# Decoder layer: ScalarE normalises all four tiles of a half in the later norms; shared experts start in the last norm; weights, route rows and down projections in a new order

## What is computed

```python
x = x + attn(layernorm(x))          # 16 heads, delta rule over 256 steps, conv, gate, Wo
x = x + xattn(layernorm(x), ctx)    # softmax(ctx Wq . ctx Wk) applied to the features
x = x + ffn(layernorm(x))           # the part that the change is about, below

scores = sigmoid(h @ gate_weight.T)                # 16 routed experts
topk_idx = best 4 of (scores + bias) within the best 2 of 4 groups
weight = scores[topk] / sum * 2.5
routed = sum over n of weight[t, n] * ((silu(h @ gate_w[n].T) * (h @ up_w[n].T)) @ down_w[n].T)
out = routed + (silu(h @ sh_gate.T) * (h @ sh_up.T)) @ sh_down.T
```

## Time and profile before

| | us |
|---|---|
| median of three runs | 598.18 |
| the profiled execution | 597.41 |
| its span, first to last instruction | 595.5 |
| TensorE busy | 557.4 (94%) |
| VectorE, ScalarE, GpSimd busy | 437.1, 398.3, 298.9 |
| mean granted TensorE clock | 0.991 |

### The profile page before, as it was taken

How to read it: one execution, slowest core, us unless ns; L and a number is a source line. 1 busy time by engine, 2 the same in 40 slices (tenths; PEclk the granted TensorE clock), 3 DMA queues, 4 the chain that set the end, 5 groups by cost and what they waited for, 6 DMA issues and landing times.

```text
span 595.5 us, 10331 instructions
## 1 busy us (share of the span) xinstructions
PE 557.4 (94%) x3392; PEld 488.2 (82%) x3392; DVE 437.1 (73%) x1046; ACT 398.3 (67%) x783; POOL 298.9 (50%) x201
## 2 busy tenths in 40 slices
PE   3899999999999999999999999897777799999996
PEld 1687889989989989989989988786566688888885
DVE  8778989989989988998998998968593433333334
ACT  4978988878978979879779778665531433343331
POOL 2434756746746646656666563301041655556542
PEclk9998999999999999999999999999998899999999
DMA  6122032032032032032031020110002433333311
GB/s 206 29 107 81 0 117 81 1 116 81 2 117 81 2 116 81 2 116 75 8 116 56 27 97 23 59 29 1 0 1 70 149 105 107 104 123 113 108 62 70
DMA packets 16267, 42.23 MB, mean 71 GB/s; under 512 B 4544, under 2 KB 4800, under 8 KB 16224
## 3 DMA queue, kind: packets, MB, share of 16 engines
q1 hardware_dynamic: 16224, 41.69, 20.9%
HBM read 40.47 MB, written 1.21 MB: 70 GB/s over the span
## 4 chain that ended last, share of the span: by engine, by line
PE 83%; DVE 8%; ACT 4%; DMA 2%; issue 2%; SPq 1%; ACTq 0%; DVEq 0%
PE bank L1258 20%; PE bank L1260 19%; PE bank L1259 19%; PE bank L1254 15%; PE bank L1396 5%; PE bank L1384 4%; ACT tok L624 2%; DMA xbias<-in_xb 1%; DMA w_raw<-in_w 1%; DVE stats L976 1%; DVE xT_lo L911 1%; DVE gated_lo L1158 1%; ACT values L538 0%; DVE x L1248 0%; DVE raw L995 0%
## 5 line engine op out<-in xcount | busy, mean ns | idle before, releaser
L1258 PE MATMUL bank<-xT_lo,w_hi 128*128 128x512 f32 x336 | 140.0, 417 | 3.6 <-DVE conv L1149 1.3
L1260 PE MATMUL bank<-xT_hi,w_hi 128*128 128x512 f32 x336 | 132.3, 394 | 0.0
L1259 PE MATMUL bank<-xT_hi,w_lo 128*128 128x512 f32 x336 | 131.8, 392 | 0.0
L425 POOL TENSOR_TENSOR gated_lo<-gated,gated_hi 128x512 fp32r<-128x512 f32 x30 | 38.7, 1290 | 116.5 <-ACT gated_hi L644 112.8
L624 ACT ACTIVATE tok<-bank,nmr,rstd 128x128 f32<-128x128 f32 x256 | 91.0, 504 | 2.1 <-DVE nmr L891 2.1
L502 POOL TENSOR_TENSOR gate<-conv,tap 128x512 f32<-128x512 f32 x36 | 46.4, 1291 | 84.5 <-DVE conv L1149 71.4
L1258 PEld LDWEIGHTS bank<-xT_lo,w_hi 128*128 128x128 f32 x336 | 63.5, 189 | 18.8 <-DVE conv L995 3.2
L1260 PEld LDWEIGHTS bank<-xT_hi,w_hi 128*128 128x128 f32 x336 | 63.3, 188 | 14.2
L420 POOL TENSOR_TENSOR conv<-tap,conv 128x506 f32<-128x506 f32 x32 | 61.9, 1934 | 21.8 <-DVE conv L995 21.8
L420 POOL TENSOR_TENSOR raw<-tap,raw 128x506 f32<-128x506 f32 x32 | 61.9, 1934 | 20.3 <-DVE raw L995 16.3
L1259 PEld LDWEIGHTS bank<-xT_hi,w_lo 128*128 128x128 f32 x336 | 63.7, 190 | 9.6
(11 more groups left out here) (167 smaller groups left out, 1358.3 us busy)
## 6 DMA issues: line engine op xcount, KB each, us to landing
w_raw<-in_w SPq DMA_DIRECT2D x34, 384.0 KB, 4.4
obet<-obet_rows SPq DMA_DIRECT2D x16, 768.0 KB, 4.2
tap<-route_rows SPq DMA_DIRECT2D x16, 512.0 KB, 3.6
wv_raw<-in_wv SPq DMA_DIRECT2D x8, 256.0 KB, 4.8
wo_raw<-in_wo SPq DMA_DIRECT2D x8, 256.0 KB, 4.9
x<-in_x SPq DMA_DIRECT2D x2, 512.0 KB, 4.6
out_x<-x SPq DMA_DIRECT2D x4, 256.0 KB, 2.4
raw<-in_ctx SPq DMA_DIRECT2D x1, 512.0 KB, 5.4
```

The lines of the kernel that those rows point to most:

```text
L425: nc.gpsimd.tensor_tensor(gated_lo[:, cc], gated[:, c * N:(c + 1) * N], gated_hi[:, cc].bitcast(F32), ALU.subtract).then_inc(gated_lo_read ...
L1258: nc.tensor.matmul(o, l_hi, r_lo, start=start, stop=False, skip_group_check=loose)
L1259: nc.tensor.matmul(o, l_lo, r_hi, start=False, stop=False, skip_group_check=loose)
L1260: return nc.tensor.matmul(o, l_hi, r_hi, start=False, stop=stop, skip_group_check=loose)
```

## The change

- In norms 2 and 3 (i = 1, 2) `half_norm` writes all four tiles of a half on ScalarE, none on VectorE.
- The second half's two energies get banks of their own (6 and 7), and their maxima and exponentials move behind the first half's norm. `context_recip` of the second half stays ahead of that half's norm factors on VectorE.
- Experts 3 and 4 get their split weights early, in buffers that are free by then (`early_high` on ScalarE ahead of the second half's softmax, `early_low` on GpSimd after the first mix has been added). Experts 5 and 6 take the two ordinary slots, which SyncE loads as soon as these are free. GpSimd then does nothing until the router chain is over (`r_ready`).
- The shared experts aren't multiplied by ones any more; their product goes straight to `act_high`.
- Activations are kept in two buffers, and `down(n)` stands two experts behind `gate_up(n)`; the first half of the shared experts' gate and up stands among the last norm's steps.
- In the loop, ScalarE and GpSimd split the gate and up weights of expert n + 1 and the down weights of expert n in step n. SyncE loads gate and up weights (256 KB) and down weights (128 KB) apart, in the order gate/up of n + 2, route row of n, down of n + 2.

The three `early`, `two` and `e_bank` helpers only pick addresses: the buffers for experts 3 and 4, the half of a double buffer by the parity of n, and the bank. `e_count(n, c)` numbers the chunks, since the shared experts' chunks run in another order.

```diff
@@ -358,35 +384,55 @@
+            for n in (5, 6):
+                sp.wait_ge(w_lo_ready, n - 2 + H)
+                load_expert(n, 1 - n % 2)
             sp.wait_ge(r_tr_ready, NCH)
             sp.dma_start(route_rows, routeT).then_inc(ld["route_rows"], 16)
             sp.wait_ge(ld["route_rows"], 16)
 
-            def load_route(e, s, before):
-
-                sp.wait_ge(e_weighted, before)
+            def load_route(e, s):
+
+                if not (isinstance(e, int) and e < 2):
+                    sp.wait_ge(e_weighted, e * NCH - NCH)
                 sp.dma_start(wbc[:, s * T:(s + 1) * T],
                              route_rows[bass.ds(e, 1), :].broadcast_to([P, T])).then_inc(ld_route[s], 16)
 
+            def load_gate_up(n, s):
+
+                sp.wait_ge(w_lo_ready, n + (H - 2))
+                m = n + (H - 1)
+                sp.dma_start(w_raw[:, s * 3 * D:s * 3 * D + 2 * D],
+                             w_in[bass.ds(m, 1), :, 0:2 * D].rearrange("a p c -> (a p) c")).then_inc(ld_w[s], 16)
+
+            def load_down(n, s):
+                sp.wait_ge(down_lo_ready, n - 6)
+                m = n + (H - 1)
+                sp.dma_start(w_raw[:, s * 3 * D + 2 * D:(s + 1) * 3 * D],
+                             w_in[bass.ds(m, 1), :, 2 * D:3 * D].rearrange("a p c -> (a p) c")
+                             ).then_inc(ld_down[s], 16)
+
+            load_route(0, 0)
+            load_route(1, 1)
+            load_gate_up(7, 0)
+            load_route(2, 0)
+            load_down(7, 0)
+            load_gate_up(8, 1)
+            load_route(3, 1)
+            load_down(8, 1)
+            with sp.Fori(0, E_ROUTED // 2 - 3) as r:
+                for s in range(2):
+                    load_gate_up(r * 2 + (9 + s), s)
+                    load_route(r * 2 + (4 + s), s)
+                    load_down(r * 2 + (9 + s), s)
             for s in range(2):
-                load_route(s, s, NCH * (s + 1))
-            with sp.Fori(0, E_ROUTED // 2 - 1) as r:
...
-            def weigh(n, s, first):
-
-                for c in range(NCH):
-                    pool.wait_ge(u_prod, (n - 1) * NCH + c + 1)
-                    if not first:
-
-                        pool.wait_ge(e_hi, (n - 2) * NCH + c + 1)
-                        pool.wait_ge(e_lo, (n - 2) * NCH + c + 1)
-                    cc = slice(c * N, (c + 1) * N)
-                    nc.gpsimd.tensor_tensor(act_w[:, cc], prod[:, cc], wbc[:, s * T + c * N:s * T + (c + 1) * N],
-                                            ALU.mult).then_inc(e_weighted, 1)
-
-
-
-            pool.wait_ge(p_added, TT // 2)
-            nc.gpsimd.memset(wbc, 1.0).then_inc(ones_ready, 1)
-            pool.wait_ge(ones_ready, 1)
-            weigh(1, 0, True)
-            gate_up_low(3, 0)
-            weigh(2, 1, False)
-            gate_up_low(4, 1)
-            down_low(3, 0)
-
-            def step(n, s, left=2):
-
-                pool.wait_ge(ld_route[s], (n - 1 - s) * 8)
-                weigh(n, s, False)
-                if left > 1:
-                    gate_up_low(n + 2, s)
-                if left > 0:
-                    down_low(n + 1, 1 - s)
-
-            with pool.Fori(0, E_ROUTED // 2 - 1) as r:
+            def early_low(n):
+                hi, lo = early(n)
+                s = 1 - n % 2
+                pool.wait_ge(w_hi_ready, n + H)
+                nc.gpsimd.tensor_tensor(lo, w_raw[:, s * 3 * D:(s + 1) * 3 * D], hi.bitcast(F32),
+                                        ALU.subtract).then_inc(w_lo_ready, 1)
+
+            def weigh(n, m, s, c):
+
+                pool.wait_ge(u_prod, n * NCH + (c + 1 - NCH))
+                if not (isinstance(n, int) and n < 5):
+
+                    pool.wait_ge(e_hi, n * NCH + (c + 1 - 3 * NCH))
+                    pool.wait_ge(e_lo, n * NCH + (c + 1 - 3 * NCH))
+                nc.gpsimd.tensor_tensor(weighted(m, c), prod[:, two(m, c)],
+                                        wbc[:, s * T + c * N:s * T + (c + 1) * N],
+                                        ALU.mult).then_inc(e_weighted, 1)
+
+
+            pool.wait_ge(x_mixed, 1)
+            early_low(3)
+            early_low(4)
+
+            pool.wait_ge(r_ready, 1)
+            gate_up_low(5, 0)
+            gate_up_low(6, 1)
+
+            def step(n, m, s, up=True, down=True):
+                pool.wait_ge(ld_route[s], n * 8 - (1 + s) * 8)
+                weigh(n, m, s, 0)
+                if up:
+                    gate_up_low(n + 1, 1 - s)
+                weigh(n, m, s, 1)
+                if down:
+                    down_low(n, s)
+
+            step(3, 3, 0, False, False)
+            step(4, 4, 1, False, False)
+            step(5, 5, 0, False)
+            step(6, 6, 1)
+            with pool.Fori(0, E_ROUTED // 2 - 3) as r:
                 for s in range(2):
-                    step(r * 2 + (3 + s), s)
-            step(E_ALL - 1, 0, 1)
-            step(E_ALL, 1, 0)
+                    step(r * 2 + (7 + s), 7 + s, s)
+            step(E_ALL - 1, E_ALL - 1, 0)
+            step(E_ALL, E_ALL, 1, False)
...
                 act.wait_ge(ln_rstd, NCH * i + c + 1)
-                for t in (G * c, G * c + 1):
+
+                for t in range(G * c, G * c + (2 if i == 0 else G)):
                     nc.scalar.activation(x_norm[:, t * D:(t + 1) * D], x[:, t * D:(t + 1) * D],
                                          ACT.Identity, scale=rstd[:, t:t + 1],
...
 
             act.wait_ge(ld["router"], 32)
             nc.scalar.activation(rw_hi, rw, ACT.Copy).then_inc(small_split, 1)
             context_soft(0)
-            context_exp((4, 5))
             context_att(0)
             half_norm(1, 0)
+            half_out(1, 0, xT)
+            context_exp((4, 5))
             context_exp((6, 7))
-            half_out(1, 0, xT)
+            early_high(3)
+            early_high(4)
             context_soft(1)
             context_att(1)
             half_norm(1, 1)
             half_out(1, 1, xT)
-            for c in range(NCH):
-                half_norm(2, c)
...
-            def step(n, s, left=2):
-                gate_silu(n, False)
-                if left > 1:
-                    gate_up_high(n + 2, s)
-                act_high(n, False)
-                if left > 0:
-                    down_high(n + 1, 1 - s)
-
-            with act.Fori(0, E_ROUTED // 2 - 1) as r:
+            def step(n, m, s, up=True):
+                gate_silu(n, m)
+                if up:
+                    gate_up_high(n + 1, 1 - s)
+                act_high(n, m)
+                down_high(n, s)
+
+            gate_silu(4, 4)
+            act_high(3, 3)
+            gate_silu(5, 5)
+            act_high(4, 4)
+            act_high(5, 5)
+            down_high(5, 0)
+            step(6, 6, 1)
+            with act.Fori(0, E_ROUTED // 2 - 3) as r:
                 for s in range(2):
-                    step(r * 2 + (3 + s), s)
-            step(E_ALL - 1, 0, 1)
-            step(E_ALL, 1, 0)
...
-            def norm_half(i, c):
+            def norm_half(c):
                 norm_factors(G, D, G * c).then_inc(ln_rstd, 1)
-                half_norm(i, c)
 
             gated_out(g, k, 0)
+            context_recip(0)
+            add_stats((0, 1), p_full, p_acc, p_added)
+            gated_out(g, k, 1)
+            norm_half(0)
             context_max(2)
-            context_recip(0)
-            add_half(0, p_full, p_acc, p_added)
-            gated_out(g, k, 1)
-            norm_half(1, 0)
             context_max(3)
-            add_half(1, p_full, p_acc, p_added)
+            add_stats((2, 3), p_full, p_acc, p_added)
             context_recip(1)
-            norm_half(1, 1)
+            norm_half(1)
             dve.wait_ge(small_split, 2)
             nc.vector.tensor_tensor(rw_lo, rw, rw_hi.bitcast(F32), ALU.subtract).then_inc(r_lo_ready, 1)
-            add_half(0, x_mix_full, mix_acc, x_mixed)
-            norm_half(2, 0)
-            add_half(1, x_mix_full, mix_acc, x_mixed)
+            add_stats((0, 1), x_mix_full, mix_acc, x_mixed)
+            norm_half(0)
+            add_stats((2,), x_mix_full, mix_acc, x_mixed)
             half_low(2, 0)
-            norm_half(2, 1)
+            add_stats((3,), x_mix_full, mix_acc, x_mixed)
+            norm_half(1)
+
...
             def half_transpose(i, c):
 
-                pe.wait_ge(ln_norm_act, 2 * (NCH * i + c + 1))
-                pe.wait_ge(ln_norm_dve, 2 * (NCH * i + c + 1))
+                if i == 0:
+                    pe.wait_ge(ln_norm_act, 2 * (c + 1))
+                    pe.wait_ge(ln_norm_dve, 2 * (c + 1))
+                else:
+                    pe.wait_ge(ln_norm_act, TT // 2 + G * (NCH * (i - 1) + c + 1))
                 for kt in range(KT):
...
             half_transpose(1, 0)
-            mix(0)
+            mix(0, (0, 1))
             context_weights(1)
             half_transpose(1, 1)
-            mix(1)
+            mix(1, (2,))
+            half_transpose(2, 0)
```

(68 more changed lines are left out.)

224 lines of the change are left out of this document (128 added, 96 removed).

## The result

| | before | after |
|---|---|---|
| median of the runs, us | 598.18 | 627.64 (3 runs, 624.64 to 627.73) |
| profiled execution: time / span, us | 597.4 / 595.5 | 624.64 / 622.9 |
| mean granted clock of TensorE | 0.991 | 0.977 |
| TensorE's busy time, share of the span | 557.4 us, 94% | 568.0 us, 91% |

The changed kernel is slower: ratio 1.0469, 95% interval 1.0386 to 1.0553. I had forecast 620 us and a range of 606 to 633.

A forecast was written before the change was run, and what follows sets the result against it. TensorE bound the old kernel; the exposed route row would bound the new loop. `down_low(5)` at 465.3, 11 turns of 11.5 to 591.8, then the last matmuls and tail: 618.8, plus 1.9 outside the span, 620.7; forecast 620 us, range 606 to 633.

The forecast's parts named there:

- its length: Router chain: falls from 19.2 to 12.2 us, 5.7 from GpSimd being idle and 1.3 from expert chunks moved out.
- `down_low(5)` ends: Before the loop: first route row, weighing, expert 5's row, rounding and both splits put this end at 465.3 us.
- R: In the loop, from the end of `down_low` to the route row's landing: 5.3 us, between 4.4 and 6.6.
- second `weigh`: GpSimd's last `weigh` in a loop step: 1.29 us, plus 0 to 0.7 for an `act_low` between, taken as 0.2.
- turn: Loop cycle between `down_low` ends: 11.5 us (10.4 to 13) where TensorE needs 8.28, repeated 11 times.
- from there to the end of the span: After the loop: 5.3 + 2.65 to `gate_up(18)`, 5.5 + 3 x 2.8 of matmuls, 1.6 slow start, 3.5 tail.
- The price of the page: Loop transfers by the skill page: 4.1 us rather than 5.1, cycle 10.5, result about 609, still inside the range.
- this stage gives nothing to the router (0.4 later): Norms and cross attention: the router chain begins at 432.3 us against 431.96, with one quarter more of gate/up done.
- rival D: TensorE's clock in the loop: pauses absorb a low clock; at 1.2 GHz throughout, the kernel takes 689 us; 3%.
- all 5.7 of the old excess: Router chain: seven long VectorE instructions each go beside a GpSimd one; with GpSimd idle there, 5.7 us go.
- A: Loop, faster: the route row lands in time, TensorE's work bounds again, experts 8.28 us apart, 581 us; 7%.
- C: Middle: VectorE's long instructions stay or ScalarE's four tiles cost more; `down_low(5)` ends 6 us later, 626; 10%.

The follow-up runs named there:

- route_early: Changed kernel with each route row issued one place earlier in SyncE's list, no longer behind the transfer that waits for the other expert's down half: 585.28 us, ratio 0.9786.
- before_late: Kernel before, with each route row issued on SyncE behind the transfer that waits for its own down-projection half: 633.44 us, ratio 1.0571.
- early_split: route_early with the tiles of the two later norms shared again, two on ScalarE and two on VectorE: 581.31 us, ratio 0.9733.
- pool_late: Changed kernel with GpSimd's two wide subtractions for experts 3 and 4 started with the router's scores, beside the router's chain: 634.99 us, ratio 1.0619.
- split_again: early_split measured once more, unchanged, with more rounds and beside the next kernel on one chip: 582.36 us, ratio 0.9733.
- tuned: early_split with ScalarE's two wide copies moved later and GpSimd's two wide subtractions placed anew among VectorE's norm ops: 578.67 us, ratio 0.9675.

## Why the prediction was right, step by step

**What decides it** held as put: the route row issued only behind `down_low`, first thing needed by the next step. route_early removes it and gives 585; before_late adds it and gives 633.

| step | forecast | measured |
|---|---|---|
| router's chain begins | 432.3 | 434.74 |
| its length | 12.2 | 12.2 |
| `down_low(5)` ends | 465.3 | 468.10 |
| end of `down_low` to the first `weigh` (R) | 5.3 | 5.37 at 484.27; mean 5.5 |
| second `weigh` | 1.29 + 0 to 0.7 | 1.74 |
| turn | 11.5 | 11.70 |
| `down_low(16)` ends | 591.8 | 596.77 |
| from there to the end of the span | 27.0 | 26.1 |
| span | 618.8 | 622.9 |

The 4.1 us between the spans are 2.8 before the loop, 2.2 in eleven turns of 0.2 each, less 0.9 at the end. The median, 627.64, lies 7.6 above the 620 that I forecast, because it is also 3.0 above the profiled execution from which these rows come.

The signs mostly held: a wait for the row in every turn, experts 11 to 12 apart, TensorE waiting in the loop for nothing but `gate_up_low`, and no op of the chain over 1 us. Two were a little off: TensorE was 79% busy from 475 to 600 (98.58 of 125 us), where I had said 72%, and the row was issued 1.35 after `down_low`'s end, where I had said 1.2 at most.

**The loop.** R was mis-sized by a little. I gave an issue 0.4; in the loop issues are 0.5 to 0.7 apart (478.93, 479.62, 480.25), and the landing behind the row's own is 3.7 to 4.2 in these two turns. Both errors cancel, which is luck: from the first issue to the landing I had 5.1, and it took 5.0 in this turn (478.93 to 483.96) and 5.3 in the next. The 0.3 from the landing to the start of `weigh` (483.96 to 484.27) I had left out. R's mean over the 12 waits behind a `down_low` is 5.5 for my 5.3; the first of the 13 waits for a row, 6.5, stands ahead of the loop. The second `weigh` takes 0.4 to 0.5 more than the first in every turn, beside an `act_low` that starts 0.5 before it and is itself longer (1.08 for 0.69): inside my 0 to 0.7.

**The price of the page.** By an estimate from the Trainium skill, DMA: Bandwidth & Descriptors, "Anatomy of one DMA", three transfers of 896 KB in all would have landed 4.1 behind the first issue. They took 5.0 to 5.3: the trace doesn't agree, and 1.3 of that are the two issues ahead of the row, which stand in no figure of one DMA.

**Before the loop.** The step "this stage gives nothing to the router (0.4 later)" failed by 2.4 us. The order of events was as I had it, and even some things came sooner (the reciprocal at 405.38, for my 406.8). What I left out is TensorE's low clock here; I had priced it behind the last wait and, as rival D, in the loop. It fell around a wait of 2.69 us for ScalarE's tiles, which ended at 412.16. ScalarE and TensorE in the changed kernel, and the window:

```profile
414.66 2.06 ACT L593 ACTIVATE values<-x,nmr,rstd 128x256 f32<-128x256 f32 x4
```

```profile
414.81 3.78 PE L1349 MATMUL bank<-attT,qk 128*128 128x256 f32 x8 [0.69 <-ACT qk L601]
418.39 1.91 PE L1367 MATMUL bank<-ident,values 128*128 128x128 f32 x8
```

```profile
415.00:420.00 5.00, 5.00 (x16) 4.17 (x17) 1.33 (x3) 2.23 (x5) 0.00 (x0) 0.50 0.00 0
```

The tiles of the third norm's first half were written at 416.72, sooner than my 417.6. TensorE was still in the mix, which took 3.78 where early_split at full clock has 1.99, and the transposes 1.91 for 1.09. Their copies were out at 420.94 for my 419.1, and the last statistics at 423.63 for 421.7, 1.9 late; of the 2.4 at the chain, 0.5 came behind that. No run changed the clock alone, so this is read from the chain of waits and from early_split.

The factors of that half were held by GpSimd too, which I had named and priced at nothing:

```profile
410.42 1.73 DVE L934 TENSOR_TENSOR nw<-stats 128x4 f32<-128x4 f32 x1
```

In this trace that cost nothing: the factors were ready at 414.32, and ScalarE began the tiles at 414.66 straight from its copies, with no wait. In route_early ScalarE did wait for them, 0.44 us.

**The router's chain.** The seven long ops of the earlier trace rows are gone: L1298 takes 0.18 and L1267 0.29; the chain is 12.2, as forecast. pool_late shows the mechanism: GpSimd's work put back beside it adds 3.2. That it made all 5.7 of the old excess is inferred from the times at which both engines end.

**The rivals.** A (581) is near to what the kernel does once the row is early, 585.28: its condition was false, and its working 4 us low, with the late start of the loop in that. Of C's 6 us at the end of `down_low(5)` 2.8 came: none of it by long instructions of VectorE, most of it in the stage of the four tiles. D did not come: the loop's clock was 0.94 from 480 to 560 (0.86 from 492 to 504), and TensorE still waited for `gate_up_low` in every turn, so its pauses absorbed it. With the row in time the change is worth 12 us (585.28 beside 597.51, ratio 0.973 to 0.9841).

## What to carry to other kernels

A queue of transfers is one list in order: a transfer that waits holds back every one behind it. So for each transfer ask not only what frees its buffer but what the entries ahead of it wait for, and keep a transfer that the next step begins with ahead of those that wait for this step's end. An engine that is busy for 47% of the span (GpSimd here) can bound a loop when its turn holds an uncovered landing of 4 us. And before wide work is moved to an idle stretch of GpSimd, look at which of VectorE's ops run there.

## What the runs showed of the hardware

- A GpSimd subtraction with both inputs in SBUF holds VectorE's small ops with two SBUF inputs until it ends (0.20 became 1.75 and 1.89) and also the normalising L986, one SBUF input and two scalars (0.73 became 2.31 and 2.32). Additions with one input in PSUM (1.28 for two) and the batch-norm statistics (1.39 for four) ran beside it unchanged. The Trainium skill, SBUF — State Buffer, "Who interferes with whom", names both kinds, two SBUF inputs and the two-port modes of VectorE, for which it gives a lock held for the whole instruction; the traces agree.
- SyncE issues the transfers of its loop 0.5 to 0.7 us apart (490.62, 491.15, 491.78), where I had reckoned with 0.4.
- TensorE's granted clock in one stretch differs between executions of the same kernel: from 410 to 420 it was 1.00 in early_split and 0.66 in split_again, with 1.4 us between the spans. In tuned the executions with a mean clock of 1.000, 0.997 and 0.994 have spans of 576.0 to 576.2, 577.6 and 578.7.
